# A decoder block on one core: the stretch between its two attentions, with projection, tile transposes and first scores in another order, and its loops written out

## The reference

```python
x = x + attn(layernorm(x))        # 32 heads of 32, 8 kv heads, weights binarised (sign), no mask
x = x + xattn(layernorm(x))       # below
x = x + ffn(layernorm(x))         # dense 1024x1024, plus a LoRA per sequence and a shared one

def xattn(h):                     # h: (2, 512, 256*4)
    y = einsum('blhc,hoc->bloh', h.reshape(2, 512, 256, 4), read_w)       # 3 outputs of 256
    q, k, v = affine(normalise_each_256(y)) @ qkv_w.T                     # one weight for each
    q, k = rope(q), rope(k)                                               # 16 heads of 16
    o = softmax(causal(q @ k.T / 4)) @ v
    ...                                                                    # rat_write, then an mlp part
```

## Time and profile before

| | |
|---|---|
| runs (3), median | 1004.54 us (1002.41 to 1006.26) |
| profiled execution, own time | 1001.63 us |
| its span, granted TensorE clock | 999.9 us, 0.913 |
| busy in the span: PE, DVE, ACT, POOL | 849.5, 661.7, 410.3, 313.4 us |
| chain that ended last | PE 60%, DVE 16%, ACT 7%, issue 6%, SPq 5%, DMA 4% |

### The profile page before, as it was taken

The page is one execution under the profiler, slowest core; times in us unless marked ns, Lnnn a source line. Parts: engine busy times, 40 slices in busy tenths (PEclk is TensorE's granted clock), DMA queues, the critical chain, the costliest instruction groups (busy, mean ns, idle before and its releaser), DMA issues.

```text
span 999.9 us, 16412 instructions
## 1 busy us (share of the span) xinstructions
PE 849.5 (85%) x5594; PEld 459.1 (46%) x5594; DVE 661.7 (66%) x1364; ACT 410.3 (41%) x795; POOL 313.4 (31%) x297
## 2 busy tenths in 40 slices
PE   4899699999899998668878589847599999999987
PEld 3574232333333433445555223216366656656643
DVE  7865458888688863476666666432677788778761
ACT  5547317667576765022122156632233323423310
POOL 2000006667666767130000035430231322322210
PEclk9999899999999999899998576866799999999997
DMA  8656422231313221202115531020000011011011
GB/s 335 253 171 173 139 73 65 84 97 51 106 43 104 87 72 38 74 6 69 37 51 167 189 88 64 27 65 1 12 1 15 28 43 29 13 42 32 1 38 47
DMA packets 75370, 75.75 MB, mean 76 GB/s; under 512 B 37233, under 2 KB 63617, under 8 KB 74658
## 3 DMA queue, kind: packets, MB, share of 16 engines
q1 hardware_dynamic: 74738, 68.71, 22.2%
q10 hardware_dynamic: 560, 6.12, 1.7%
HBM read 53.56 MB, written 21.04 MB: 75 GB/s over the span
## 4 chain that ended last, share of the span: by engine, by line
PE 60%; DVE 16%; ACT 7%; issue 6%; SPq 5%; DMA 4%; POOL 2%; DVEq 0%; POOLq 0%; ACTq 0%; PEldq 0%
PE psum L1953 6%; PE psum L1533 6%; PE psum L1890 5%; PE psum L1615 5%; PE psum L1668 4%; PE psum L1735 4%; PE psum L1875 3%; PE psum L1656 3%; PE psum L1679 3%; PE psum L1835 2%; DMA ops<-q_scr 2%; PE psum L1728 2%; PE psum L1938 2%; PE psum L1777 2%; DVE m_neg L1199 2%
## 5 line engine op out<-in xcount | busy, mean ns | idle before, releaser
L1199 DVE TENSOR_REDUCE m_neg<-psum 128x1 f32<-128x512 f32 x256 | 164.5, 681 | 55.0 <-PE psum L1615 53.0
L869 ACT ACTIVATE region_x<-psum 128x512 f32<-128x512 f32 x256 | 140.7, 597 | 72.7 <-PE psum L1656 72.5
L663 POOL TENSOR_TENSOR region_p<-region_x 128x2048 f32<-128x2048 f32 x32 | 145.1, 4535 | 46.2 <-ACT region_x L869 28.1
L1615 PE MATMUL psum<-ops 96*128 96x512 f16 x256 | 97.6, 390 | 18.3 <-DMA ops<-q_scr 13.8
L1656 PE MATMUL psum<-ops 98*128 98x512 f16 x256 | 96.6, 384 | 1.8 <-ACT region_x L869 1.7
L1533 PE MATMUL psum<-region_x,region_w 128*128 128x512 f16 x320 | 76.6, 397 | 3.0 <-ACT region_w L805 3.0
L1615 PEld LDWEIGHTS psum<-ops 96*128 96x128 f16 x256 | 24.9, 98 | 98.9 <-DVE m_neg L1199 69.0
L1953 PE MATMUL psum<-ynT,region_w 128*128 128x128 f32 x512 | 63.7, 289 | 6.3 <-ACT ynT L1023 6.3
L1668 PE MATMUL psum<-region_x,v_g 128*32 128x512 f32 x512 | 67.8, 604 | 0.0
L1953 PEld LDWEIGHTS psum<-ynT,region_w 128*128 128x128 f32 x512 | 62.1, 204 | 10.0 <-ACT ynT L1023 10.0
L1728 PE MATMUL psum<-sign_o_all,region_a 128*128 128x512 f16 x256 | 60.6, 387 | 1.4 <-PEq L1741 1.4
(11 more groups left out here) (217 smaller groups left out, 1510.3 us busy)
## 6 DMA issues: line engine op xcount, KB each, us to landing
ops<-q_scr SPq DMA_DIRECT2D x48, 128.0 KB, 2.4
region_a<-in_x SPq DMA_DIRECT2D x8, 512.0 KB, 8.3
region_a<-in_w_q SPq DMA_DIRECT2D x8, 512.0 KB, 6.6
region_w<-in_w_o SPq DMA_DIRECT2D x8, 512.0 KB, 4.0
region_w<-in_kern SPq DMA_DIRECT2D x16, 256.0 KB, 2.8
kern_scr<-region_w SPq DMA_DIRECT2D x32, 128.0 KB, 1.8
region_p<-in_x SPq DMA_DIRECT2D x8, 512.0 KB, 3.3
region_a<-kern_scr ACTq DMA_DIRECT2D x1, 4096.0 KB
```

The costliest lines, as they stand in the source:

```text
L663: pool.tensor_tensor(pair_sum[:, n], prob_a[:, 2 * n], prob_a[:, 2 * n + 1], ALU.add).then_inc(pair_ready, 1)
L869: act.activation(prob_a[:, kt, j, :], psum[:, (0, 4, 5)[(16 * k + n) % 3], :], ACT.Exp, scale=A_SCALE).then_inc(p_ready, 1)
L1199: dve.tensor_reduce(m_neg[:, k % 3, n:n + 1], psum[:, 1 + (16 * k + n) % 3, :], AX_X, ALU.max, negate=True).then_inc(s_max, 1)
L1615: pe.matmul(psum[:, 1 + (16 * k + n) % 3, :], qa_op[u][0:A_MAX, j, qt * P:(qt + 1) * P], k_op[u][0:A_MAX, :], start=True, stop=True).then_ ...
```

## The change

1. `out_proj` runs one tile further ahead: both halves of tile 1 and one of tile 2 come before the first round, and round i does (i + 2, 1), cut at OP_ROT = 4 by the rotated transposes, and (i + 3, 0).
2. The next tile is transposed right behind yn's transposes (`turn_tile(i + 1)`), ahead of qkv. qkv goes to banks 6 and 7, the rotated tile to bank 2.
3. VectorE's order is `rope(i - 1)`, `read(i)`, `split(i - 1)`, `residual(i + 2)`.
4. The 16 scores of step 0 of the second attention lie in rounds 5 to 7 (X_FILL) and use two banks; their transpose of the maxima is in round 7, ahead of its qkv; four scores of step 1 come ahead of the last rotated transposes.
5. The rows of ones in `ops` come by two DMAs from a small tile of ones. In v_x only the columns of ones are filled: tiles 2 to 7 before the first attention, tiles 0 and 1 after it.
6. All loops of the first attention and of this stretch are written out, with constant addresses and semaphore values.
7. SyncE loads x up to four tiles ahead, and loads heads before a round's store, not after it.

```diff
-OP_HT, OP_YN = 8, 15
+OP_ROT = 4
...
+        def x_score_bank(i, m):
+            return m % 2 if i == 0 else (16 * i + m) % 3
+
+        X_FILL = {5: ((), (), range(0, 2)), 6: (range(2, 3), range(3, 4), range(4, 10)), 7: (range(10, 11), range(11, 12), range(12, 16))}
...
-            with sp.Fori(0, A_ROUNDS) as t:
-                for k in range(2, 2 + OPS):
-                    load_qk(t, k + 2)
-                    load_max(t, k + 1)
-                    store_kern(t, k)
-                    load_kern(t * OPS + k + 1)
...
+            for k in range(2, NI - 2):
+                load_qk(k + 2)
+                load_max(k + 1)
+                store_kern(k)
+                load_kern(k + 1)
...
+            for i in range(2, 4):
+                sp.wait_ge(x1_ready, i - 1)
+                load_x(i, i % 2)
             for i in range(NT - 1):
-                if i + 2 < NT:
-                    sp.wait_ge(x1_ready, i + 1)
-                    load_x(i + 2, i % 2)
-                store_qk(i)
                 if i == NT // 2:
-                    sp.wait_ge(made, 17)
                     sp.wait_ge(qk_stored, 192 * (NT // 2) + 192)
                 if i >= NT // 2:
                     load_heads(i - NT // 2)
+                store_qk(i)
+                if i + 4 < NT:
+                    sp.wait_ge(x1_ready, i + 3)
+                    load_x(i + 4, i % 2)
+                if i == 0:
+                    for a in (0, 64):
+                        sp.dma_start(ops[a + X_MAX:a + X_ROWS, XI * 2 * S:], ones[:]).then_inc(xm_loaded, 16)
...
+            pool.memset(v_ones[:, 2:], 1.0)
...
-            pool.memset(v_x, 1.0).then_inc(made, 1)
...
+            pool.memset(v_ones[:, 0:2], 1.0).then_inc(made, 1)
...
-                    for r in (32, 96):
-                        pool.memset(ops[r:r + 32, XI * 2 * S:].bitcast(F32), ONES).then_inc(made, 1)
...
+            copy_turned(0)
+            for i in range(NT):
+                if i > 0:
                     rotated_hi(i - 1)
...
+                if i + 1 < NT:
+                    copy_turned(i + 1)
+                else:
+                    x_max_hi(0)
...
+                if i == NT - 2:
+                    load_later()
...
+            residual(0)
+            residual(1)
+            for i in range(NT):
+                if i > 0:
+                    rope(i - 1)
+                read(i)
+                if i > 0:
+                    split(i - 1)
+                if i + 2 < NT:
+                    residual(i + 2)
+                if i == min(X_FILL):
+                    dve.wait_ge(made, 17)
+                for part in X_FILL.get(i, ()):
+                    for m in part:
+                        x_maximum(0, m)
+            x_max_lo(0)
             rope(NT - 1)
+            for m in range(4):
+                x_maximum(1, m)
             split(NT - 1)
...
+            def turn_tile(i):
+                pe.wait_ge(h_ready, i + 1)
+                pe.wait_ge(r_lo, i)
+                turn(2, h_st, KC, hT_mm)
...
-            def x_round(i, first=False, last=False):
-                pe.wait_ge(h_ready, i + 1)
-                turn(2, h_st, KC, hT_mm)
-                if not last:
-                    out_proj(i + 1, 0, 0, OP_HT)
...
+            def x_round(i):
                 pe.wait_ge(hT_ready, 2 * i + 2)
-                pe.wait_ge(vx_ready, i + 1)
-                pe.wait_ge(rope_step, 6 * i + 6)
                 for c in range(KC):
                     mm = pe.matmul(psum[:, 4 + c // 4, (c % 4) * 3 * HC:(c % 4 + 1) * 3 * HC], hT[:, c, :], read1[:, c, :], start=True, stop=True)
                 mm.then_inc(y_mm, 1)
...
+                x_fill(i, 0)
+                if i + 2 < NT:
+                    out_proj(i + 2, 1, 0, OP_ROT)
+                if i > 0:
                     turn_rotated(i - 1)
...
+                x_fill(i, 1)
+                if i + 2 < NT:
+                    out_proj(i + 2, 1, OP_ROT)
                 pe.wait_ge(yn_ready, 6 * i + 6)
...
+                pe.wait_ge(vx_ready, i + 1)
                 turn(6, yn, 6, ynT_mm)
...
+                if i + 1 < NT:
+                    turn_tile(i + 1)
+                if i + 3 < NT:
+                    out_proj(i + 3, 0)
+                x_fill(i, 2)
+                if i == NT - 1:
+                    x_turn_max(0)
                 pe.wait_ge(ynT_ready, 6 * i + 6)
...
+            for h in range(2):
+                out_proj(1, h)
+            turn_tile(0)
+            out_proj(2, 0)
+            pe.wait_ge(att_hi_ready, NI)
+            pe.wait_ge(att_lo_ready, NI + 1)
+            pe.wait_ge(xw_loaded, 16 * 6)
+            for i in range(NT):
+                x_round(i)
+            for m in range(4):
+                if m == 0:
+                    pe.wait_ge(r_lo, NT)
+                x_score(1, m)
             turn_rotated(NT - 1)
...
+            for m in range(4, X_LEAD):
+                x_score(1, m)
```

More of the change, by code:

```diff
@@ L692, in _ @@
             pool.wait_ge(trig_done, 4)
-            values(0, 0)
-            step(0, 0, done=0)
-            step(0, 1, done=1)
-            with pool.Fori(0, A_ROUNDS) as t:
-                for k in range(2, 2 + OPS):
-                    step(t, k)
-            step(0, NI - 2)
-            step(0, NI - 1, last=True)
-            pair(0, NI - 1, 1)
+            values(0)
+            step(0, done=0)
+            step(1, done=1)
+            for k in range(2, NI - 2):
+                step(k)
+            step(NI - 2)
+            step(NI - 1, last=True)
+            pair(NI - 1, 1)
             pool.wait_ge(att_lo_ready, NI + 1)
@@ L1325, in split @@
                 dve.wait_ge(r_hi, i + 1)
-                dve.tensor_tensor(lo_st[:], psum[:, 6, :], hi_st[:], ALU.subtract).then_inc(r_lo, 1)
-            dve.sem_inc(rT_mm, 1)
-            residual(0, 0, 1, None)
-            read(0)
-            residual(1, 1, 1, 1)
-            rope(0)
-            with dve.Fori(0, NT // 2 - 1) as it:
-                for u in range(2):
-                    i = it * 2 + 1 + u
-                    read(i)
-                    split(i - 1)
-                    residual(i + 1, u, it + 2, i + 1)
-                    rope(i)
+                dve.tensor_tensor(lo_st[:], psum[:, 6 if i == NT - 1 else 2, :], hi_st[:], ALU.subtract).then_inc(r_lo, 1)
             def x_maximum(i, m):
@@ L1689, in spread_inverse, with step @@
                 mm.then_inc(den_spread, 1)
-            def step(t, k, done=3, left=2):
+            def step(k, done=3, left=2):
                 for n in range(16):
                     if n < 16 - LEAD and left > 0:
-                        score(t, k + 1, n + LEAD)
+                        score(k + 1, n + LEAD)
                     if n >= 16 - LEAD and left > 1:
-                        score(t, k + 2, n + LEAD - 16)
-                    shifted(t, k, n)
+                        score(k + 2, n + LEAD - 16)
+                    shifted(k, n)
                     if n == 1 and done > 1:
-                        spread_inverse(t, k - 2)
+                        spread_inverse(k - 2)
                     if n in (2, 4, 6) and done > 0:
-                        values(t, k - 1, n // 2)
+                        values(k - 1, n // 2)
                     if n in (7, 10) and done > 0:
-                        denominators(t, k - 1, n // 10)
+                        denominators(k - 1, n // 10)
                     if n == 8 and left > 0:
-                        turn_max(t, k + 1)
+                        turn_max(k + 1)
                     if n == 14:
-                        values(t, k, 0, last=left == 0)
-            step(0, 0, done=0)
+                        values(k, 0, last=left == 0)
+            step(0, done=0)
             pe.wait_ge(qk_lo, NI + 4)
             pe.wait_ge(made, 14)
-            step(0, 1, done=1)
+            step(1, done=1)
             pe.wait_ge(made, 14)
-            with pe.Fori(0, A_ROUNDS) as t:
-                for k in range(2, 2 + OPS):
-                    step(t, k)
+            for k in range(2, NI - 2):
+                step(k)
             for i in (NI - 2, NI - 1):
-                step(0, i, left=NI - 1 - i)
-            spread_inverse(0, NI - 2)
+                step(i, left=NI - 1 - i)
+            spread_inverse(NI - 2)
             for n in range(3):
-                values(0, NI - 1, 1 + n)
+                values(NI - 1, 1 + n)
             def out_proj(i, h, begin=0, end=2 * KC):
```

403 lines of the change are left out of this document (175 added, 228 removed).

## The result

The changed kernel takes **974.76 us** (median of 4 runs, 972.35 to 975.68), the kernel before beside it 1003.47 (4 runs, 999.63 to 1006.26): ratio 0.9684, 95% interval 0.9651 to 0.9717. Predicted were 979.5 us, 971 to 992, and faster. The profiled execution fell from 1001.63 to 975.68 us (span 973.7, granted clock 0.913 in both).

What follows compares the result with a forecast made beforehand. First attention bound by TensorE's pace; between the attentions, waits worth removing. Gains of 8 us there and 17.0 us between sum to 25.0, from 1001.63 to 976.6 for that execution, 979.5 as a median; range 971 to 992.

Steps and rivals of the forecast that it cites:

- SyncE's constants: First attention: constant addresses let q land 0.8 us earlier in four steps; 3 us taken, bounds 0 and 7.2.
- rival C: Last rounds keep the 2.4 GHz level: rounds 6 and 7 take 16.1 and 15.9, 974 to 976 us; chance 0.12.
- The branch: First attention: writing out the loop removes the step's whole excess at the branch back, 5.0 us; bounds 2.43 and 5.0.
- rival D: Slower: straight code is fetched late, 5.0 us per miss; five misses cancel the gain, seven make 1014; chance 0.06.
- rival A: The first attention keeps its stalls on q: 982 to 985 us; chance 0.25 together with the 17 us rounds.
- Start: Start of the stretch between the attentions: y(0) begins 3.1 us later than before, with more projection behind it.
- First round: First round between the attentions: 15.1 us instead of 20.85, with fills replaced by two small DMAs.
- Middle rounds: Rounds 1 to 4 between the attentions: 16.1 us each instead of 17.2 to 18, TensorE standing 1.7.
- Rival B: The rounds between the attentions keep 17 us: 985.5 us; chance 0.25 together with the kept stalls on q.
- Rounds 5 to 7: Last rounds between the attentions: 13.9, 17 and 18.3 us, the last at the lower clock.
- To the first shifted score: From the last qkv to the second attention's first shifted score: 8.8 us instead of 11.5.
- rival E: The change does little: heads or hi_st late in rounds 5 to 7, gain some 5 us; chance 0.07.

Runs made afterwards that it cites:

- b2: The kernel before with only SyncE's loop of the first attention written out, the other engines' loops kept; 1006.07 us, ratio 0.9977 to the kernel before.
- c1: The changed kernel with extra matmuls, which nothing reads, in TensorE's idle time of the last two rounds; 976.36 us, ratio 0.9707 to the kernel before.
- c2: The changed kernel with SyncE's load_max(2) right behind the stores of tile 7 and store_y(0); 971.70 us, ratio 0.9671 to the kernel before.
- d0: The changed kernel itself, run again in another group with a second trace; 977.32 us, ratio 0.9685 to the kernel before.
- c4: The changed kernel with the next tile's transposes put behind qkv again; 982.08 us, ratio 0.9772 to the kernel before.
- b3: The kernel before with all loops written out, in both stretches, in the old order of the rounds; 1000.25 us, ratio 0.9924 to the kernel before.
- b4: The kernel before, all loops written out, plus two DMAs of ones and small v_x fills, old order; 991.20 us, ratio 0.9877 to the kernel before.
- d1: The changed kernel with extra matmuls, SyncE's load_max(2) earlier, and kern loaded as four 1 MB loads in the second attention; 977.13 us, ratio 0.9680 to the kernel before.
- c3: The changed kernel with the 4 MB load of kern moved to step 4 of the second attention; 983.65 us, ratio 0.9778 to the kernel before.

## Why the prediction was right

The sign and the range held, and the parts of the change paid in the way forecast, but for SyncE's constants. The time came out 4.7 us under the 979.5 forecast, just outside the 4 us that I gave my own sum. It lies in the 974 to 976 of rival C, but not by C's mechanism: round 6 ran at the low clock. The gain ahead of the second attention was larger than forecast (31.8 for 25.0), and the 5.6 lost behind it, no more than two traces of one kernel differ by, brought the total near: that part is luck.

1. **The branch, 5.0 us.** Right to 0.1 (19.69 to 14.67), and b2 puts it on the computing engines. The straight code shows no gap of issue over 0.7 us up to the last stage, so the late fetch of rival D did not come. The Trainium skill (Runtime: NRT & Kernel Launch, Instruction fetch mechanics) says that prefetch is purely sequential, and that a taken branch whose target is outside the two pages held stalls on a fetch; the trace agrees.
2. **SyncE's constants, 3 us.** The number came (2.9 in b2), the mechanism did not: q was to land 0.8 earlier in each of four steps. It goes out 0.6 earlier, but 2.8 of the 2.9 are in one step, with one late q, and the other three gain nothing. I had not seen that this step alone, 18.25, held half of the 7.2 us of stalls. The stage gained 9.3 in all up to the first out_proj, for 8 predicted, so rival A is out.
3. **Start.** y(0) was to come 3.1 later than before, 1.5 of it for the low clock. After: 1.5 later, without the low clock; in c1, c2, d0 and c4, 2.8 to 3.2 later, with it. (32 matmuls at 0.22 are 7.0 us, not the 6.9 of the sum.)
4. **First round, 15.1.** 14.5. The fills, which I priced at VectorE's 3.3, cost 5.5 with TensorE's clock (b3 to b4).
5. **Middle rounds, 16.1.** Mis-sized: 15.24 in all four. I laid groups of matmuls end to end by their durations, but these overlap by up to 0.17 us at each joint: the two groups of transposes take 1.6 (2.0), qkv 2.6 (2.9). Yn's transposes begin at +7.6 (7.8 forecast, though its own terms, 0.2 + 2.56 + 4.9, add up to 7.7). The waits were as predicted: one, 1.7 forecast, 1.65 measured. Part of the gain is also the short loops, 0.35 a round, which I had at nothing (b3). Rival B (17 us) is out.
6. **Rounds 5 to 7: 13.9, 17, 18.3.** 13.5, 18.95, 16.6. Round 6 runs at the low clock nearly throughout (that case I had put at 1.5 longer; it is 1.95). Round 7 begins at 2.4 GHz again (y 1.92, where I took 3.70), so yn comes at +7.6 and not at +8.9.
7. **To the first shifted score, 8.8.** 9.3. The sum was wrong: its terms (2.8, 5.8 less three maxima, 0.6) add up to 7.8.

The stretch so gained 22.6 us (20.9 in d0), not 17.0: terms 3 to 5 were too careful by 1.7, 0.6 and 3.4. In term 6 two misses nearly cancelled: round 6 took 1.95 more than forecast, rounds 5 and 7 took 2.1 less.

Of the signs of being wrong one came: ScalarE waited for SyncE's stores before hi_st of tile 7, for 0.9 us, beside the 4 MB load. The prediction had given hi_st slack at the landing time of a q load and left that load out. No score waited for a load of heads, so rival E is out.

The step "nothing is given back" failed as a statement on this execution: 5.6 us were. 3.5 of it are in the second attention. 1.9 of these are the wait for load_max(2), behind 23 issues of SyncE; I had looked at TensorE's order there and not at what SyncE does between two loads of maxima. But that wait is 1.11 in d0 and 3.63 in b4, so even this part is not shown to come of the change. What is left is no more than two traces of the same kernel differ by.

## What to carry to other kernels

Cost a stage in start-to-start times, and cost an idle of TensorE twice: for itself and for the low clock on the work behind it. Before a stage is made faster, look at which small transfers its new timing brings beside a large one, since they can take about as long as it does to land. And when stages that nobody touched differ between two traces by a fixed step, run the same kernel again before explaining it.

## What the runs showed that I had not expected

- A 32 KB DMA is held up beside a 4 MB one on another queue: about 13.5 us until the stores have landed (c1; in d1, without the load, they are no longer waited for 2.0 us after the last issue), and 8.4 instead of 2.1 (c3).
- The spread of this kernel's runs goes with TensorE's clock. Over the 43 runs of the kernel before in the three groups, time and mean granted clock have a correlation of -0.86, and 0.01 of clock is about 5 us (least squares over these runs). Which of the two follows from the other is not shown.
- Short hardware loops cost 0.35 us a round on a chain that changes engines, with no gap that a single row shows.
